# Rotary tiles as separate tasks for q and k, banks returned by the last turn instruction, clip on GpSimd

## The reference, cut to what matters

```
xn = layernorm(x)
out = x + attention(xn) + local_transformer(xn)

attention: qkv = xn @ W_qkv + b_qkv; 16 heads of 64; causal softmax(q k^T / 8) v; @ W_out + b_out

local_transformer, 2 layers, each:
  h = shift_token(x)                       # the second half of the features comes from the token before
  q, k, v = split(h @ wqkv)                # 8 heads of 64
  q = q / clip(norm(q), 1e-12) * q_scale;  k likewise with k_scale
  q = q * cos * s + rotate_half(q) * sin * s;  k likewise with 1 / s     # rotary
  x = x + softmax(window of 128 keys)(8 q k^T) v @ wo
  h = layernorm(shift_token(x)) * g + b
  x = x + (a * gelu(gate)) @ w2 + b2,  a, gate = split(h @ w1 + b1)
```

## Time and profile before

| | |
|---|---|
| timed runs, median | 3817.17 us |
| the profiled execution, its own time | 3824.69 us |
| span of that execution | 3822.8 us |
| mean granted TensorE clock | 0.966 |
| TensorE matmul busy | 3278.0 us, 86% |
| VectorE busy | 2101.3 us, 55% |
| ScalarE busy | 1694.2 us, 44% |
| GpSimd busy | 983.3 us, 26% |

### The profile page before, as it was taken

One profiled execution on the slowest core, in us unless ns is written; L12 is line 12 of the kernel. 1 busy time (PEld: TensorE's weight loads), 2 busy tenths in 40 slices (PEclk: granted clock), 3 DMA queues, 4 the chain that ended last, 5 costly groups with the idle time before them and its releaser, 6 DMA issues.

```text
span 3822.8 us, 96024 instructions
## 1 busy us (share of the span) xinstructions
PE 3278.0 (86%) x35300; PEld 2174.9 (57%) x35300; DVE 2101.3 (55%) x7233; ACT 1694.2 (44%) x3181; POOL 983.3 (26%) x743
## 2 busy tenths in 40 slices
PE   1689898898989889898988989889898988979898
PEld 0356465565656556465655646566565655656565
DVE  2365564646556464654647556464655646465464
ACT  1245354444535354453544535344453534445354
POOL 2141230403223041321404133140412304132140
PEclk9799999999999999999999999999999999999999
DMA  3000000000000000000000000000000000000000
GB/s 79 1 7 2 10 2 10 2 2 10 2 10 2 10 2 2 10 2 10 2 5 7 2 10 2 10 2 2 10 2 10 2 10 2 2 7 2 7 2 4
DMA packets 42627, 26.49 MB, mean 7 GB/s; under 512 B 13266, under 2 KB 40828, under 8 KB 42108
## 3 DMA queue, kind: packets, MB, share of 16 engines
q1 hardware_dynamic: 42108, 19.59, 1.8%
HBM read 14.96 MB, written 4.19 MB: 5 GB/s over the span
## 4 chain that ended last, share of the span: by engine, by line
issue 43%; PE 28%; DVE 16%; POOL 6%; ACT 4%; SPq 1%; DMA 0%; DVEq 0%; POOLq 0%; ACTq 0%; PEldq 0%
PE bank L1093 4%; PE bank L1179 3%; DVE ss L925 3%; PE bank L1136 3%; POOL rnorm L652 3%; DVE scratch L920 3%; PE bank L1011 3%; PE bank L1122 2%; PE bank L1194 2%; DVE scratch L922 2%; DVE bank L865 2%; ACT scratch L757 2%; DVE scratch L923 2%; PE bank L1114 1%; DVE bank L880 1%
## 5 line engine op out<-in xcount | busy, mean ns | idle before, releaser
L652 POOL TENSOR_TENSOR rnorm<-ssc,minus_half 128x8 f32<-128x8 f32 x264 | 484.7, 1836 | 997.1 <-DVE ssc L927 994.6
L865 DVE CUSTOM_DVE_ANT_0 bank<-bank,future 128x128 f32<-128x128 f32 (+3 forms) x1024 | 467.0, 527 | 145.6 <-PE bank L1055 143.6
L880 DVE CUSTOM_DVE_ANT_0 bank<-bank,band 128x192 f32<-128x192 f32 x1056 | 341.3, 394 | 277.2 <-PE bank L1074 265.7
L723 ACT ACTIVATE probs<-bank 128x512 f32<-128x512 f32 (+1 forms) x768 | 347.0, 530 | 205.4 <-PE bank L1101 205.2
L1093 PE MATMUL bank<-Qa,Ka 64*128 64x512 f32 (+3 forms) x2048 | 395.1, 465 | 44.5 <-DVE ss L925 36.5
L1136 PEld LDWEIGHTS bank<-Va,probs 128*64 128x64 f32 x10240 | 338.8, 144 | 117.2 <-issue 107.4
L757 ACT ACTIVATE scratch<-bank 128x512 f32<-128x512 f32 x264 | 158.7, 601 | 512.0 <-DVE ss L925 286.1
L1136 PE MATMUL bank<-Va,probs 128*64 128x65 f32 x10240 | 375.2, 231 | 0.7
L641 POOL TENSOR_TENSOR lrstd<-lvar,minus_half 128x4 f32<-128x4 f32 x33 | 33.4, 1013 | 1308.1 <-DVE lvar L943 1308.1
L1179 PE MATMUL bank<-Lqkv,resid 128*128 128x512 f32 x528 | 289.2, 674 | 32.6 <-ACT resid L746 23.5
L731 ACT ACTIVATE lprobs<-bank 128x384 f32<-128x384 f32 x528 | 226.8, 491 | 199.0 <-PE bank L1124 195.5
(11 more groups left out here) (144 smaller groups left out, 7148.9 us busy)
## 6 DMA issues: line engine op xcount, KB each, us to landing
x_res<-in_L_attn_x SPq DMA_DIRECT2D x16, 256.0 KB, 2.9
x_rows<-in_L_attn_x SPq DMA_DIRECT2D x16, 256.0 KB, 3.1
out<-yT SPq DMA_DIRECT2D x16, 256.0 KB, 2.7
Lqkv<-in_L_ffn_wqkv SPq DMA_DIRECT2D x2, 768.0 KB
yT<-in_L_attn_W_qkv SPq DMA_DIRECT2D x6, 256.0 KB, 2.7
rope_t<-in_rope SPq DMA_DIRECT2D x8, 128.0 KB
Lw<-in_L_ffn_w SPq DMA_DIRECT2D x2, 341.0 KB
Lwo<-in_L_ffn_wo SPq DMA_DIRECT2D x2, 256.0 KB
```

What stands on the lines that cost most here:

```text
L652: g.tensor_tensor(rnorm[s][:, :], ssc[s][:, :], minus_half[:, :], ALU.pow).then_inc(rnorm_ready.sem, 1)
L723: psum.raise_read(a.activation(probs[j][:, at:at + n], psum.bank(task, (u, j))[:, 0:n], ACT.Exp, scale=float(HEAD) ** -0.5), task, (u, j))
L865: ins = v.tensor_tensor_reduce(psum.bank(task, (u, j))[:, at:at + n], psum.bank(task, (u, j))[:, at:at + n], future[:, SEQ - n:SEQ], 1.0, ...
L880: ins = v.tensor_tensor_reduce(psum.bank(task, (u, j))[:, k * BAND:(k + 1) * BAND], psum.bank(task, (u, j))[:, k * BAND:(k + 1) * BAND], b ...
```

## The change

f_qk becomes two tasks, f_q and f_k, and f_qkt becomes f_qt and f_kt, in the order of tasks, in the planner's costs and needs, in the ring of banks and on every engine. The ROTARY distance holds for f_q alone. f_k needs f_q of its tile, f_q of layer 1 needs the last f_k of layer 0. On VectorE the bank is given back by the last of the three products; the sum of squares raises a signal of its own, `sums_ready`, and ss is kept for q and k apart. The clip moves to GpSimd, which waits for that signal. The probability and maxima tasks claim both banks of a step at once, with one set of waits. Some waits are now carried by a semaphore increment on the waiting engine (`carried`).

```diff
-F_FRONT = [("f_qk", 0), ("f_v", 0), ("f_qk", 1), ("f_qkt", 0), ("f_v", 1), ("f_qk", 2), ("f_v", 2),
-           ("f_qkt", 1), ("f_qk", 3), ("f_v", 3), ("f_qkt", 2), ("f_qkt", 3)]
+F_FRONT = [("f_q", 0), ("f_k", 0), ("f_v", 0), ("f_q", 1), ("f_qt", 0), ("f_k", 1), ("f_kt", 0), ("f_v", 1),
+           ("f_q", 2), ("f_qt", 1), ("f_k", 2), ("f_kt", 1), ("f_v", 2), ("f_q", 3), ("f_qt", 2), ("f_k", 3), ("f_kt", 2),
+           ("f_v", 3), ("f_qt", 3), ("f_kt", 3)]
...
-    "f_qk": (0.9, [("act", 1.2, 0.0), ("dve", 5.2, 0.6), ("pool", 7.0, 2.9)], 2),
+    "f_q": (0.45, [("act", 0.6, 0.0), ("dve", 2.9, 0.0), ("pool", 2.9, -0.7)], 2),
+    "f_k": (0.45, [("act", 0.6, 0.0), ("dve", 2.2, 0.0), ("pool", 4.2, 0.0)], 2),
...
-    "f_qkt": (0.9, [("act", 1.25, 0.0)], 1),
+    "f_qt": (0.45, [("act", 0.6, 0.0)], 1),
+    "f_kt": (0.45, [("act", 0.6, 0.0)], 1),
...
+        "f_q": lambda: [("f_k", 0, TILES - 1)] if at[0] else [("f_first",)],
+        "f_k": lambda: [("f_q", *at)],
...
     def claim(self, engine, i, task, mark, after=()):
-        slot, k = self.use[task, mark]
-        last = {slot: k - 1}
+        return self.claims(engine, i, task, [mark], after)[0]
+
+    def claims(self, engine, i, task, marks, after=()):
+        uses = [self.use[task, mark] for mark in marks]
+        last = {slot: k - 1 for slot, k in uses}
         for u in after:
             last[self.use[u][0]] = max(self.use[u][1], last.get(self.use[u][0], 0))
...
 # GpSimd
+                        pool.wait_ge(sums_ready.sem, sums_ready.now(i, task, c))
+                        pool.sem_inc(carried["pool"], 1)
+                        g.tensor_scalar(ssc[:, :], ss[s][:, :], 1e-24, None, ALU.max).then_inc(clip_ready.sem, 1)
+                        pool.wait_ge(clip_ready.sem, clip_ready.now(i, task, c))
+                        g.tensor_tensor(rnorm[s][:, :], ssc[:, :], minus_half[:, :], ALU.pow).then_inc(rnorm_ready.sem, 1)
...
 # ScalarE
+                        t0, prev = earlier(task, lambda t: t[0] in ("f_q", "f_k"))
+                        act.wait_ge(sums_ready.sem, (sums_ready.before if prev else sums_ready.now)(i, t0, t0[0][2]))
+                        act.sem_inc(carried["act"], 1)
+                        psum.wait_filled(act, i, task, c)
+                        a.activation(squares, psum.bank(task, c)[:, :], ACT.Square).then_inc(squares_ready.sem, 1)
...
 # VectorE
+                        v.tensor_tensor(heads(turn_a), src, table(0, 0, HEAD), ALU.mult)
+                        tb = heads(turn_b)
+                        v.tensor_tensor(tb[:, :, 0:hh], src[:, :, hh:HEAD], table(1, 0, hh), ALU.mult)
+                        psum.raise_read(v.tensor_tensor(tb[:, :, hh:HEAD], src[:, :, 0:hh], table(1, hh, HEAD), ALU.mult), task, c)
...
+                        v.tensor_reduce(ss[s][:, :], heads(squares), AX.X, ALU.add).then_inc(sums_ready.sem, 1)
+                        if c == "q":
+                            t0, prev = earlier(task, lambda t: t[0] == "f_k")
+                            dve.wait_ge(qk_ready.sem, (qk_ready.before if prev else qk_ready.now)(i, t0, "k"))
+                            dve.sem_inc(carried["dve"], 1)
                             psum.wait_read(dve, i, task, c)
+                            v.tensor_tensor(turned, turn_a, turn_b, ALU.add).then_inc(turned_ready[c].sem, 1)
...
 # TensorE
+                    elif kind in ("f_qt", "f_kt"):
+                        c = kind[2]
+                        pe.wait_ge(qk_ready.sem, qk_ready.now(i, (kind[:3], *task[1:]), c))
+                        pe.sem_inc(carried["pe"], 1)
+                        transposes(i, task, c, lambda t: qkn["qk".index(c)][:, tile(t)])
```

More of the change, by code:

```diff
@@ L133, in needs @@
         return [((kind[:2] + "pv", *at, 1), 9)]
-    if kind == "f_qkt":
-        return [(("f_qk", *at), 9)]
+    if kind in ("f_qt", "f_kt"):
+        return [((kind[:3], *at), 9)]
     if kind == "f_max" and at[1] == 0:
-        return [(("f_qkt", at[0], t), 1) for t in range(TILES)] + ([(("f_ot", 0, LPAIRS - 1), 9)] if at[0] else [])
+        return [((turned, at[0], t), 1) for t in range(TILES) for turned in ("f_qt", "f_kt")] + ([(("f_ot", 0, LPAIRS - 1), 9)] if at[0] else [])
     return [(t, 9) for t in {
@@ L308, in claim @@
             engine.wait_ge(self.read[other], i * self.per_slot[other] + (self.per_slot[other] + n))
-        return self.banks[slot]
+        return [self.banks[slot] for slot, _ in uses]
     def raise_filled(self, ins, task, mark):
@@ L463, in prenorm_attention_and_local_transformer @@
                     [sem(f"bank{k}_read") for k in range(RING)], dict(
-            a_proj="qk", a_v="v", a_neg="m", a_ot="o", f_first="h", f_qk="qk", f_v="v", f_qkt="qk", f_neg="m", f_ot="o",
+            a_proj="qk", a_v="v", a_neg="m", a_ot="o", f_first="h", f_q="q", f_k="k", f_v="v", f_qt="q", f_kt="k", f_neg="m", f_ot="o",
             f_wo="w", f_mean="c", f_var="v", f_rep="r", f_gate=(0, 1, 2), f_up="a", f_down="w", out="t", xt="x",
@@ new lines, in steps, with table @@
+                        c = kind[2]
+                        s = "qk".index(c)
+                        dve.wait_ge(squares_ready.sem, squares_ready.now(i, task, c))
+                        dve.sem_inc(carried["dve"], 1)
+                        src = heads(psum.bank(task, c))
+                        def table(term, a, b):
+                            return rope_t[:, l, 2 * s + term, t, a:b].unsqueeze(1).broadcast_to([P, LHEADS, b - a])
+                        t0, prev = earlier(task, lambda t: t[0] in ("f_q", "f_k"))
@@ L1087, in steps @@
                         for u, (_, _, uses) in enumerate(CAUSAL_USES):
-                            bank = [psum.claim(pe, i, task, (u, j), after if u == 0 else []) for j in range(2)]
+                            bank = psum.claims(pe, i, task, [(u, j) for j in range(2)], after if u == 0 else [])
                             for k, at in uses:
@@ L1168, in steps @@
                         transposes(i, task, "h", lambda t: h[:, t, :])
-                    elif kind == "f_qk":
+                    elif kind in ("f_q", "f_k"):
                         _, l, t = task
-                        if t == 0:
+                        if kind == "f_q" and t == 0:
                             if l == 0:
@@ L1176, in steps @@
                             pe.sem_inc(carried["pe"], 1)
-                        for c, m in enumerate("qk"):
-                            bank = psum.claim(pe, i, task, m)
-                            psum.raise_filled(mm(bank[:, :], resid[l][:, tile(t)], Lqkv[l][:, c * INNER:(c + 1) * INNER], start=True,
-                                                 stop=True), task, m)
+                        c = "qk".index(kind[2])
+                        bank = psum.claim(pe, i, task, kind[2])
+                        psum.raise_filled(mm(bank[:, :], resid[l][:, tile(t)], Lqkv[l][:, c * INNER:(c + 1) * INNER], start=True,
+                                             stop=True), task, kind[2])
                     elif kind == "f_v":
```

136 lines of the change are left out of this document (53 added, 83 removed).

## The result

| | before | after |
|---|---|---|
| median of 8 runs | 3817.30 us (3812.23 to 3832.41) | 3827.41 us (3823.73 to 3839.34) |
| ratio, 95% interval | | 1.0027 (1.0015 to 1.0039) |
| profiled execution | 3824.69 us | 3823.73 us |
| span, granted clock | 3822.8 us, 0.966 | 3821.6 us, 0.956 |
| TensorE busy | 3278.0 us | 3326.8 us |

The kernel became slower by 10 us, where 64 us less were forecast. What follows reads where the time went from the two profiles, and checks the part of the clock on all timed executions, since the granted clock differs from one execution of a kernel to the next (0.963 to 0.974 in 24 of before).

The account below looks back on a forecast made before the run. TensorE, busy 86% of the span, was taken to bound the kernel. Per sequence 1.5 + 0.5 + 5.5 + 0 + 0.8 - 3.0 - 1.3 = 4.0 us, 64 us in 16, gave 3753 us; forecast's own range 3700 to 3809, overall 3645 to 3855.

Parts of the forecast that it names:

- Two tasks: negfT: TensorE's wait for ScalarE's copy of negfT, 2.4 us a sequence, loses between 0 and 2.4; 1.5 taken.
- Two tasks: the negation: The negation's wait behind the maxima, 1.4 us a sequence, loses between 0 and 1.4; 0.5 taken.
- The bank: Earlier return of the rotary bank cuts TensorE's 7.9 us of waits a sequence by 3.4 to 7.9; 5.5 taken.
- The last transposes of a front: TensorE waits for qn at a front's end: 0 to 7.4 us a sequence lost; 3.0 taken.
- A new order, other gaps: Reordering all 160-odd tasks makes waits the old order avoided: 0 to 5 us a sequence lost; 1.3 taken.
- The clock: Half-speed stretch after the stops at pair 1's maxima and the negation may go: up to 1.7 us a sequence; 0.8 taken.
- Rival 4: f_k straight after f_q, so the split does not separate: -0.5 us a sequence, within rival 2; chance 0.10 together.
- Rival 2: Gains and new waits of 4 to 6 us cancel: 3817 us; chance 0.10 together with rival 4.
- Rival 3: Transposes placed too early, everything waits for qn, 7.4 us a sequence: 3881 us; chance 0.20.
- The clip on GpSimd: 264 clips, 127 us, leave VectorE; each takes GpSimd 0.15 us plus 0.33 between steps; qn and kn path 0.5 us longer.
- The lock between two engines: VectorE and GpSimd block each other on shared SBUF ports; the clip can stand behind VectorE's turned add (0.69 us).
- Claims together: 37 fewer waits a sequence on TensorE's sequencer: between 1.9 us gained and 0.8 lost; 0 taken.

Follow-up runs that it names:

- e2: Changed kernel with only two tasks moved later in the order, the last q transposes of layer 0 and last k transposes of layer 1: 3775.3 us, 0.9871 of before.
- e5: Changed kernel with the planner's costs and leads for f_q and f_k set from the trace, the planner writing the order: 3767.4 us, 0.9866 of before.
- e11: Kernel before with only the banks of a step claimed together: 3821.2 us, 1.0008 of before.
- e1: Changed kernel with the written task order of the kernel before: 3806.9 us, 0.9959 of before.
- e4: Changed kernel with the clip back on VectorE, behind the sum: 3816.4 us, 0.9983 of before.
- e9: Changed kernel with four extra matmuls ahead of TensorE's wait for qn in layer 0: 3814.6 us, 0.9990 of before.

## Why the prediction was wrong

Per sequence, in the profiled executions:

| step | forecast | measured |
|---|---|---|
| Two tasks: negfT | -1.5 | -2.4 |
| Two tasks: the negation | -0.5 | -1.4 |
| The bank | -5.5 | -4.2 |
| The last transposes of a front | +3.0 | +6.0 |
| A new order, other gaps | +1.3 | -1.4 |
| sum of idle time | -3.2 | -3.35 |
| The clock, TensorE's busy time | -0.8 | +2.4 |
| period | -4.0 | -0.95 |

The idle sum came out by luck, out of terms that did not: the gains in the three waits were 8.0 for 7.5, and the transposes cost twice the forecast because in layer 0 attention did not stand in between. The working had it, f_qt 3 reached 4.0 us after f_q 3 began and qn done at 7.7; measured are 3.7 and 7.84. The error was the choice "under the middle, since attention offers work at nearly every point". Rival 4 falls: ScalarE's wait went from 2.17 to 101.4 / 132 = 0.77 us a tile, the sign that the two tasks do separate. Rival 2 gave nearly the time (3817), but not by its way: waits did not cancel waits, busy time did. Rival 3 named the cause, and e2 and e5 show it, but it decided by the length of the wait, and by length alone the change would still have gained 3.35 us a sequence.

The step that failed is "The clock". It assumed that the stop at the maxima of pair 1 goes and that half speed goes with it: the gain was a term of up to -1.7, and a loss was given no bound. The stop only became shorter, half speed still follows it in 14 of 15 periods (72 us became 48), and 96 us of half speed stand behind the new waits for qn and kn, which the step "The last transposes" counted by their length alone. Busy time, forecast at -0.8 us a sequence, came out at +2.4. That is 3.2 us a sequence, 48 us in 15. The term was also misread: the earlier trace rows show 7.0 us at 0.51 and not 3.4. The second thing is not in the sum at all: the first sequence, forecast at -4.0 like the others, came 13.1 us later, all of it busy time at a clock of 0.89 (58 us at half speed became 96). That is 17 us. 48 + 17, less 2 us of better idle time, are the 63 us between the forecast and the profiled execution.

The other steps. "The clip on GpSimd": VectorE's busy time fell by 141 us (forecast 120), GpSimd's rose by 53 (40 to 130). The clip takes 0.37 us, not 0.15; the power became 0.17 us shorter:

```profile
L658 POOL TENSOR_SCALAR ssc<-ss 128x8 f32<-128x8 f32 x264 | 98.0, 371 | 1007.2 <-DVE ss L931 983.5 <-POOL qn L672 23.7
L660 POOL TENSOR_TENSOR rnorm<-ssc,minus_half 128x8 f32<-128x8 f32 x264 | 439.8, 1666 | 22.0
```

It was 1836 ns in before, so 264 x (0.371 - 0.170) = 53 us. "The lock between two engines": the clip of q stands behind the turned add, alone it is short, as one clip of each kind shows, with VectorE's add first:

```profile
1158.15 0.68 DVE L937 TENSOR_TENSOR scratch<-scratch 128x512 f32<-128x512 f32 x1
```
```profile
1147.97 0.24 POOL L658 TENSOR_SCALAR ssc<-ss 128x8 f32<-128x8 f32 x1 [0.35 <-POOL qn L672]
```

The clip at 1158.43 takes 0.50 and ends 0.10 us after the add; that at 1147.97 takes 0.24. The Trainium skill (SBUF — State Buffer, "SBUF: two separate sides") forecasts such blocking of a GpSimd instruction that reads SBUF by a VectorE one with two SBUF inputs; the trace agrees. "Claims together" at 0 is confirmed by e11. Of the signs named three failed: L926 is waited for 3.7 us a sequence and not under 3, the clock beside the maxima of pair 1 falls, and TensorE's busy time is 3326.8 us and not near 3280, the sign that mattered. The wait for qn is 4.26 us where up to 3.7 was named. The period, 225.7 us, stayed inside the bounds that were to show the forecast wrong (218 to 226), since they leave out the first sequence.

Open. What sets whether a stop is followed by half speed: all 16 stops of 4.26 us are, none of 0.83 us is, and those for lT, 1.66 us each, are in one kernel and not in the other; the same edit, the clip, moves half-speed time by +60, +1, -55 and -74 us in four orders, which I could not forecast in any. Of the 2.4 us more busy time a sequence in the profiled executions, half speed pays 1.1 (15.9 us of it in a period for 13.7) to 1.4 (TensorE is busy in 14.9 and 12.1 us of it); the rest is not explained. The 13 us at the start follow after's order (e1 417.8, e4 432.4), but which tasks cause them was not separated. And the planner's costs were changed together in e5: how much the lead and how much the length gave is not known.

## What to carry to other kernels

Where TensorE is busy near nine tenths, write the sum of a change in two lines, idle time and busy time at the granted clock, and give the second bounds on both sides that are as wide as the first: here they moved against each other by 50 us each. Take the clock from all timed executions, not from the profiled one alone: in before it ranges from 0.963 to 0.974, 84 us at half speed. After a task is split, take the parts' costs and leads from the trace, q's product here is 7.8 us behind its projection and the planner had 2.65, before judging the split: with them the planner writes an order that is 1.6% faster than after's (e5). And test a side edit in the order that it will ship in, since the sign of one (the clip) changed with the order.

## What the runs showed of the hardware

Work put in the place of a wait can make the kernel faster: 62 us more matmuls in e9 took 13 us off. All 16 stops of 4.26 us were followed by TensorE at half speed, and none once they were filled to 0.83 us. A fp32 product of 128x512 shows as two instructions, 0.88 us for both at the full clock. Thirty-seven fewer waits a sequence on TensorE's sequencer, in 21 fewer instructions of 51 ns, changed nothing (1.0008). In all kernels without added matmuls the span is idle time, plus half of the time at half speed, plus 3142 to 3167 us.
